# Attention over 1,024 positions on one core: the first-score pass as two 64-row matmuls, one in each row half of the array

## The reference

```python
xr = x.reshape(B, C, S).transpose(0, 2, 1)
qkv = (xr @ w_qkv + b_qkv).reshape(B, S, N_HEADS, 3 * d_k)
q, k, v = jnp.split(qkv, 3, axis=-1)
attn = jnp.einsum('bihd,bjhd->bijh', q, k) * scale
attn = jax.nn.softmax(attn, axis=2)
out = jnp.einsum('bijh,bjhd->bihd', attn, v).reshape(B, S, N_HEADS * d_k)
out = out @ w_proj + b_proj
return out.transpose(0, 2, 1).reshape(B, C, H, W) + x
```

## Time and profile before

| | |
|---|---|
| median of 3 runs | 4190.05 us (4183.49 to 4191.85) |
| the profiled execution | 4186.1 us, its span 4183.9 us |
| granted TensorE clock, mean | 0.982 |
| TensorE busy | 3972.2 us, 95% of the span |
| its weight loads | 3383.7 us, 81% |
| VectorE, ScalarE, GpSimd busy | 78%, 70%, 74% |

### The profile page before, as it was taken

How to read it: one execution, slowest core, us unless ns; L and a number is a source line. 1 busy time by engine, 2 the same in 40 slices (tenths; PEclk the granted TensorE clock), 3 DMA queues, 4 the chain that set the end, 5 groups by cost and what they waited for, 6 DMA issues and landing times.

```text
span 4183.9 us, 77099 instructions
## 1 busy us (share of the span) xinstructions
PE 3972.2 (95%) x18464; PEld 3383.7 (81%) x18464; DVE 3242.8 (78%) x4382; ACT 2929.9 (70%) x5527; POOL 3076.6 (74%) x2436
## 2 busy tenths in 40 slices
PE   4999999999999999999999999999999999999997
PEld 3878878888887887878878788787888878788885
DVE  3888878788787887878878788787878778787884
ACT  2777767677676776767767677676777767677774
POOL 1788777777677876777777777777777767787775
PEclk9999999999999999999999999999999999999999
DMA  6344433434343344333434344343343434334432
GB/s 179 92 109 108 132 97 92 123 101 121 97 119 95 102 133 105 107 103 98 129 100 112 101 102 118 102 135 96 95 120 104 121 95 110 105 102 124 117 82 70
DMA packets 263566, 455.18 MB, mean 109 GB/s; under 512 B 107920, under 2 KB 118160, under 8 KB 258960
## 3 DMA queue, kind: packets, MB, share of 16 engines
q1 hardware_dynamic: 263056, 449.48, 40.1%
HBM read 206.58 MB, written 41.42 MB: 59 GB/s over the span
## 4 chain that ended last, share of the span: by engine, by line
PE 84%; issue 6%; POOL 4%; DVE 2%; ACT 1%; DMA 1%; SPq 1%; POOLq 0%; DVEq 0%; ACTq 0%
PE ps_g L396 23%; PE s L418 10%; PE st L471 10%; PE ps_o L528 10%; PE ps_o L530 10%; PE st L469 10%; PE ps_g L412 9%; POOL p_hl L752 2%; PE st L515 1%; PE st L516 1%; POOL x_l L736 1%; DVE acc L653 1%; DVE nm L656 1%; ACT p_hl L592 0%; DMA rinv_d<-r 0%
## 5 line engine op out<-in xcount | busy, mean ns | idle before, releaser
L752 POOL TENSOR_TENSOR p_hl<-p,p_hl 128x512 fp32r<-128x512 f32 x2048 | 2607.6, 1296 | 1036.4 <-ACT p_hl L592 1035.6
L589 ACT ACTIVATE p<-st 128x512 f32<-128x512 f32 x2048 | 1231.1, 601 | 798.9 <-PE st L471 650.0
L656 DVE TENSOR_REDUCE nm<-s 128x1 fp32r<-128x1024 f32 x1024 | 1251.0, 1222 | 426.2 <-PE s L418 409.7
L653 DVE TENSOR_TENSOR acc<-acc,p 128x512 f32<-128x512 f32 x1792 | 1235.5, 689 | 137.3 <-issue 123.4
L592 ACT ACTIVATE p_hl<-st 128x512 fp32r<-128x512 f32 x2048 | 1236.9, 604 | 0.0
L469 PE MATMUL st<-q,k 128*128 128x512 f32 x2048 | 799.8, 391 | 17.5 <-issue 17.3
L528 PE MATMUL ps_o<-p_hl,v_hl 128*128 128x512 f32 x2048 | 805.6, 393 | 5.2 <-POOL p_hl L752 4.5
L471 PE MATMUL st<-q,k 128*128 128x512 f32 x2048 | 803.5, 392 | 0.0
L530 PE MATMUL ps_o<-p_hl,v_hl 128*128 128x512 f32 x2048 | 802.5, 392 | 0.0
L396 PE MATMUL ps_g<-x_h,wq 128*128 128x512 f32 x2016 | 715.8, 395 | 29.9 <-POOL x_l L736 29.8
L418 PE MATMUL s<-k,q 128*128 128x512 f32 x2048 | 655.4, 401 | 83.0 <-DVE nm L656 80.6
(11 more groups left out here) (79 smaller groups left out, 3714.9 us busy)
## 6 DMA issues: line engine op xcount, KB each, us to landing
wq<-wq_d SPq DMA_DIRECT2D x128, 512.0 KB, 5.1
k<-qk_h SPq DMA_DIRECT2D x256, 256.0 KB, 4.3
wv<-wv_d SPq DMA_DIRECT2D x32, 1024.0 KB, 5.1
q<-qk_h SPq DMA_DIRECT2D x128, 256.0 KB, 3.8
q<-qk_l SPq DMA_DIRECT2D x128, 256.0 KB, 4.9
k<-qk_l SPq DMA_DIRECT2D x128, 256.0 KB, 5.2
q<-q SPq DMA_DIRECT2D x256, 128.0 KB, 4.0
rinv<-rinv_d SPq DMA_DIRECT2D x256, 128.0 KB, 2.8
```

The source lines that it names most:

```text
L589: nc.scalar.activation(p[:, to, :], st[slot % RING][:], ACT.Exp)
L653: nc.vector.tensor_tensor(acc[:], acc[:], probs, ALU.add).then_inc(acc_done, 1)
L656: nc.vector.tensor_reduce(nm[:, it:it + 1], s1[:], AXX, ALU.max, negate=True).then_inc(max_done, 1)
L752: nc.gpsimd.tensor_tensor(p_l[:, to, :], p[:, to, :], p_h[:, to, :].bitcast(f32), ALU.subtract).then_inc(pl_done, 1)
```

## The change

The first-score pass takes high queries by high keys alone, over 64 rows instead of 128. Its two matmuls now lie in different row halves of the array: the first 512 keys are multiplied in rows 0 to 63, the other 512 in rows 64 to 127, each with the weights of the same 128 queries. The compiled matmuls of L418 go from a tile of 128 by 128 at (0, 0) to tiles of 64 by 128 at (0, 0) and at (64, 0); all others stay at 128 by 128.

For that the operands are stacked anew: `k1` is high above and low below, `q1` is high in both halves, `k2` has high keys below and `q2` low queries below. The sum over the two score matmuls is the same. `q2` now has two buffers and is filled by `move_head`, which has 6 transfers; `fill_q2` and its waits are gone. `sum_row` is gone to make room, and the sum goes through a row of `rinv`; ScalarE's wait for `row_stored` before that copy is gone as well.

```diff
-    MOVES = 5
+    MOVES = 6
...
-        q2 = sb("q2", [P, S], f32r)
+        q2 = [sb(f"q2_{i}", [P, S], f32r) for i in range(2)]
...
-        sum_row = sb("sum_row", [P, HALF])
...
                 for dst, src in ((k1[i][0:D, :], qk_h[D:P, :]), (q1[i][0:D, :], qk_h[0:D, :]),
-                                 (k1[i][D:P, :], qk_h[D:P, :]), (q1[i][D:P, :], qk_l[0:D, :]),
-                                 (k2[i][D:P, :], qk_l[D:P, :])):
+                                 (k2[i][D:P, :], qk_h[D:P, :]), (q1[i][D:P, :], qk_h[0:D, :]),
+                                 (k1[i][D:P, :], qk_l[D:P, :]), (q2[i][D:P, :], qk_l[0:D, :])):
                     sp.dma_start(dst.bitcast(f32), src.bitcast(f32)).then_inc(moved[i], 16)
-
-            def fill_q2(head, n):
-                sp.dma_start(q2[D:P, cols(n)].bitcast(f32), q1[head % 2][0:D, cols(n)].bitcast(f32)
-                             ).then_inc(q2_filled[n], 16)
...
-                    if u == 4 and B.on(h + 1, HEADS):
-                        sp.wait_ge(st_done, at(SLOTS, B.slot(U - 1, 1) + 1))
-                        fill_q2(h + 1, 0)
...
-                        sp.dma_start(sum_d[n:n + 1, :], sum_row[32 * n:32 * n + 1, :]).then_inc(row_stored[n], 16)
+                        sp.dma_start(sum_d[n:n + 1, :], rinv[rows.start:rows.start + 1, n, :]
+                                     ).then_inc(row_stored[n], 16)
...
             def first_scores(head, it):
-                for n in range(NH):
-                    mm = nc.tensor.matmul(s1[:, cols(n)], q1[head % 2][:, it // 4 * HALF + it % 4:(it // 4 + 1) * HALF:4],
-                                          k1[head % 2][:, cols(n)], start=True, stop=True)
-                return mm
+
+                queries = slice(it // 4 * HALF + it % 4, (it // 4 + 1) * HALF, 4)
+                nc.tensor.matmul(s1[:, cols(0)], q1[head % 2][0:D, queries], k1[head % 2][0:D, cols(0)],
+                                 start=True, stop=True)
+                return nc.tensor.matmul(s1[:, cols(1)], q1[head % 2][D:P, queries], k2[head % 2][D:P, cols(1)],
+                                        start=True, stop=True)
...
-                            pe.wait_ge(q2_filled[n], at(16 * HEADS, 16 * (h + 1)))
...
-                            nc.tensor.matmul(st[slot % RING][:], k2[i][:, keys], q2[:, cols(n)],
+                            nc.tensor.matmul(st[slot % RING][:], k2[i][:, keys], q2[i][:, cols(n)],
...
-                        if (v := at(16 * HEADS, 16 * (half // 2))) is not None:
-                            act.wait_ge(row_stored[n], v)
                         act.wait_ge(st_done, at(SLOTS, slot + 1))
-                        nc.scalar.copy(sum_row[32 * n:32 * n + 1, :], st[slot % RING][32 * n:32 * n + 1, :]
-                                       ).then_inc(st_free, 1)
+                        nc.scalar.copy(rinv[row, half % 2, :], st[slot % RING][row, :]).then_inc(st_free, 1)
```

More of the change, by code:

```diff
@@ L192, in attention_kernel @@
         moved = [sem(f"moved{i}") for i in range(2)]
-        q2_filled = [sem(f"q2_filled{i}") for i in range(NH)]
         s1_done = sem("s1_done")
@@ L260, in store_max, with load_max @@
                              ).then_inc(max_stored[n], 16)
-            def load_max(n):
-                sp.dma_start(q2[0:1, cols(n)].bitcast(f32), max_d[n:n + 1, :]).then_inc(max_loaded[n], 16)
+            def load_max(head, n):
+                sp.dma_start(q2[head % 2][0:1, cols(n)].bitcast(f32), max_d[n:n + 1, :]).then_inc(max_loaded[n], 16)
             def load_wq(head):
@@ L314, in _ @@
             load_wq(2)
-            sp.wait_ge(moved[0], 16 * MOVES)
-            fill_q2(0, 0)
             sp.wait_ge(max_done, 4)
@@ L319, in _ @@
             sp.wait_ge(max_stored[0], 16)
-            load_max(0)
+            load_max(0, 0)
             def body(B):
@@ L325, in body @@
                     h, u = divmod(U, IT)
-                    if u == 0 and B.now:
+                    if u == 0 and B.on(h + 1, HEADS):
                         if (v := at(SLOTS, B.slot(U - 1, 1) + 1)) is not None:
@@ L330, in body @@
                             sp.wait_ge(l_done, QK0)
-                        if B.on(h + 1, HEADS):
-                            move_head(h + 1)
-                        fill_q2(h, 1)
+                        move_head(h + 1)
                     if u == 0 and B.on(h + 3, HEADS):
@@ L341, in body @@
                         sp.wait_ge(max_stored[1], at(16 * HEADS, 16 * (h + 1)))
-                        load_max(1)
-                    if u == 4 and B.on(h + 1, HEADS):
-                        sp.wait_ge(st_done, at(SLOTS, B.slot(U - 1, 1) + 1))
-                        fill_q2(h + 1, 0)
+                        load_max(h, 1)
                     if u == 6 and B.on(h + 1, HEADS):
@@ L350, in body @@
                         sp.wait_ge(max_stored[0], at(16 * HEADS, 16 * (h + 2)))
-                        load_max(0)
+                        load_max(h + 1, 0)
                     if U % 4 == 2 and B.on(half := (U - 6) // 4, HALVES):
-                        n = half % 2
+                        n, (rows, _) = half % 2, half_rows(half)
                         sp.wait_ge(st_free, at(SLOTS, B.sum_slot(half) + 1))
-                        sp.dma_start(sum_d[n:n + 1, :], sum_row[32 * n:32 * n + 1, :]).then_inc(row_stored[n], 16)
+                        sp.dma_start(sum_d[n:n + 1, :], rinv[rows.start:rows.start + 1, n, :]
+                                     ).then_inc(row_stored[n], 16)
                     if U % 4 == 3 and B.on(half := (U - 7) // 4, HALVES):
@@ L609, in body @@
                     if U % 4 == 1 and B.on(half := (U - 5) // 4, HALVES):
-                        slot, n = B.sum_slot(half), half % 2
-                        if (v := at(16 * HEADS, 16 * (half // 2))) is not None:
-                            act.wait_ge(row_stored[n], v)
+                        slot, (rows, _) = B.sum_slot(half), half_rows(half)
+                        row = slice(rows.start, rows.start + 1)
                         act.wait_ge(st_done, at(SLOTS, slot + 1))
-                        nc.scalar.copy(sum_row[32 * n:32 * n + 1, :], st[slot % RING][32 * n:32 * n + 1, :]
-                                       ).then_inc(st_free, 1)
+                        nc.scalar.copy(rinv[row, half % 2, :], st[slot % RING][row, :]).then_inc(st_free, 1)
                     if U in X_SPLIT and B.ahead:
@@ L658, in _ @@
             nc.vector.memset(ones[:].bitcast(f32), 1.0)
-            nc.vector.memset(q2[0:D, :].bitcast(f32), 0.0)
             for i in range(2):
+                nc.vector.memset(q2[i][0:D, :].bitcast(f32), 0.0)
                 nc.vector.memset(k2[i][0:D, :].bitcast(f32), 0.0)
```

## The result

The changed kernel takes 4385.34 us in the median of 4 runs (4384.57 to 4387.98), the kernel before 4188.37 us in runs on the same chip; the ratio is 1.0472, with a 95% interval from 1.0454 to 1.0490. It is 197 us slower, where the prediction had 113 us less as the likeliest case. 4385 lies inside the stated range, between the first rival (4297) and the second (4676).

The account below looks back on a forecast made before the run. TensorE's stream was taken as the bound: −241 us for the pair side by side, +116 for switches, +12 given back, −113 against 4186.1, so 4073, or 4077 us as median. Range 3965 to 4480 us.

Parts of the forecast that it names:

- first rival: At each tile-shape switch the next matmul waits until the one ahead ended, weights loaded ahead: +107, 4297 us; chance 0.20.
- second rival: At each tile-shape switch the weight loads wait too: 379 us on top of 4297, giving 4676 us; chance 0.15.
- What bounds the kernel: TensorE's stream bounds the whole run; its 72.1 us of waits for VectorE's maximum belong to the loop end, unchanged.
- The pair side by side: First-score pair in two row halves holds the array as long as one matmul: 0.235 us less, 241 us over 1024.
- The weights: Strided loads of the first-score pair run at the same time, hidden by the last score matmul ahead: no cost.
- rival 3: In the first-score pass the halves do not run side by side: gain 0, 4190 to 4306 us; chance 0.19.
- The switch of the tile: Shape changes before and after each first-score pair: 0 to 0.71 us possible, 0.113 us a unit taken, 116 us.
- a third of the 0.34: Share taken of 0.34 us a unit, the two switches' cost if each waits for the matmul ahead to end.
- The moves: Sixth transfer in `move_head` lands before the next head's first pass, hidden by two units of matmuls: cost nothing.
- The sum: Whole kernel: −241 +116 +12 = −113 against the profiled 4186.1 us, 4073; 4077 us as median.

Follow-up runs that it names:

- two memset runs: Kernel before plus one small VectorE memset of an unread tile: ahead of the loop 4106.46 us (ratio 0.9818), behind the loop 4185.81 us (1.000).
- the run with half a pass: Kernel before with one of the two first-score matmuls left out in all blocks but the first: 4037.13 us, ratio 0.9643.
- layout run: Changed kernel with its first-score pass over all 128 rows again, everything but the tile kept: 4132.97 us, ratio 0.9880 to the kernel before.

## Why the prediction was wrong

*What bounds the kernel*: right that TensorE does; the switches came through to the end nearly in full, 252 us of the 285 to 287 that the stream shows. Wrong that the loop end belonged to the loop and "no first-score pass can change them". No pass did; by the two memset runs one added VectorE instruction ahead of the loop is enough, and the change has one. The prediction had looked at that edit only for its duration.

*The pair side by side*: right. Starts 0.01 us apart, and 210 us lost when both went to one half. Its worth of 217 us net (229 with a costly switch) was too high; the run with half a pass gives 150. Too little was given back: 12 to 24 us against 91.

*The weights*: right that the loads of the two halves run at the same time, which settles rival 3. Wrong that they are "hidden by that matmul". They start with the pair itself, 0.32 us behind the start of the last score matmul.

*The switch of the tile*: this is the step that failed. I took 0.113 us a unit, "a third of the 0.34", for the wait of the matmuls alone. The trace after has 0.515: 0.175 us of waiting for the two changes, about half of the 0.34 that I had as the end of that part, and 0.34 us of loads in the open, for which I had worked out 0.37 from the start of the program. The second rival had the mechanism right and its load price nearly so; its wait was twice too long, so its 4676 was too high. I gave it 0.15. The rows could not decide whether a load waits for a switch, but they had its price, and the term for it was left at nothing without a reason. Picking the value "nearest" to changes of bank and operand had no ground, since none of those rows contains a change of shape.

The Trainium skill, page "TensorEngine Tiling (Array Packing)", section "Key Properties", says that a change of the tiling mode drains TensorE, which spoke against the change. The trace after agrees that a change of shape holds the stream back: 0.32 us from start to start instead of 0.23, in four kernels, whatever runs inside the shape. It is less than a wait for the end of the matmul ahead: L460 starts at 2001.50 and ends, as the profile models it, at 2001.89, and L407 starts at 2001.82. The Trainium skill, page "TensorE: Matmul & The Clock Gate", Part 3, has some 4 ns between the starts of tiles in different row groups. The trace agrees, with 0.00 to 0.01 us.

*The moves*: not nothing, but 15.7 us in the layout run and 17.2 with half a pass; 3.4 us in the changed kernel, where the stream is slower.

*The sum*, with what was measured: −52 us for layout and code, +252 for the tile, +200 against 197. It comes out because the layout run stands between the two kernels; it tests nothing. From the trace the tile is +285 to +287, and the 35 us between are settled in part. A plain head bears the price in full: 32.53 us against the layout run's 30.24, 0.286 a unit. In the same two heads of each batch that gained nothing with half a pass, the growth is only 0.9 to 1.0 us instead of 2.3; the head with the turn grows by 3.8. By span less busy time TensorE is idle for 148.9 us in the changed kernel and for 164.3 in the layout run, 15 us less, and the layout run's profiled execution was 6 us under its median. The rest is open.

That 4385 lies inside the range is in part luck: the range had no gain at the loop end in it, and no case of the prediction, at the price that it states, gives this number.

## What to carry to other kernels

Two 64-row matmuls, one in each row half, did run side by side, but each change of tile shape cost a wait of about 0.09 us here and left the next weight load uncovered, 0.11 us for a contiguous one and 0.23 for a strided one: 0.5 us for a round trip against 0.235 won. Such a pair pays only if several pairs follow each other in one shape, here more than two for each round trip by this arithmetic; that was not tried. And when a comparison of two kernels does not add up, compare the instruction packets and look at the turn of the loop before explaining the rest.

## What the runs showed that I had not expected

One instruction ahead of a hardware loop changed the time by 80 us of 4186 (1.9%): a stall of some 9.5 us on VectorE at each of 13 turns (123.4 us in all), each with 6.8 us of TensorE at its lower clock. Why the place of that instruction decides stays open. A strided weight load costs 121 ns only where it lies open; in the stream it costs 0.013 us a matmul (27 us over 2048), by the run of the kernel before with contiguous queries.
